# A second other order for the attention steps of a decoder layer, from the 81st step on

## The reference, cut to what matters

```python
x = x + self_attention(layernorm(x), w_qkv, w_out)      # x: (4, 1024, 256) fp32, 16 heads of 16
x = x + cross_attention(layernorm(x), ctx, mask, ...)   # ctx: (4, 77, 256), q, k, v with biases
x = x + ffn(layernorm(x), ...)                          # 704 wide, SiLU gate, values and weights rounded to 8 bits

# self_attention: windows of 128 queries, each over its own 128 keys and the 128 before, causal
scores = einsum('bhcqd,bhckd->bhcqk', qc, kcat) / HD ** 0.5
attn = softmax(where(mask, scores, -inf))
out = einsum('bhcqk,bhckd->bhcqd', attn, vcat) @ w_out
# cross_attention: softmax over 77 keys, masked by mask_SxS2_ik0
# ffn: the rounding scale of its input is max |layernorm(x)| over the whole tensor
```

## Time and profile before

| | us |
|---|---|
| median of 3 runs | 680.71 |
| lowest, highest | 676.21, 681.20 |
| the profiled execution | 682.17 |
| its span on the core | 680.4 |

### The profile page before, as it was taken

The page is one execution under the profiler, slowest core; times in us unless marked ns, Lnnn a source line. Parts: engine busy times, 40 slices in busy tenths (PEclk is TensorE's granted clock), DMA queues, the critical chain, the costliest instruction groups (busy, mean ns, idle before and its releaser), DMA issues.

```text
span 680.4 us, 20176 instructions
## 1 busy us (share of the span) xinstructions
PE 623.9 (92%) x8115; PEld 398.6 (59%) x8120; DVE 513.1 (75%) x984; ACT 403.1 (59%) x601; POOL 166.6 (24%) x215
## 2 busy tenths in 40 slices
PE   2999999999998999999999998999997999888885
PEld 2557575867665666566757664566754645333364
DVE  6698777777877767557866875677669778699897
ACT  3335666775674557566555466445354683899692
POOL 2004332432343210240242022123102011345300
PEclk9999999999999999999999998998999999999999
DMA  7744134562344243437323353434247340000024
GB/s 258 185 149 148 46 114 118 145 158 67 112 123 127 81 124 84 112 115 181 108 60 113 113 147 72 116 81 127 70 119 213 85 84 2 1 0 1 1 93 155
DMA packets 58266, 71.61 MB, mean 105 GB/s; under 512 B 23819, under 2 KB 35263, under 8 KB 58175
## 3 DMA queue, kind: packets, MB, share of 16 engines
q1 hardware_dynamic: 54495, 68.36, 36.1%
q10 hardware_dynamic: 3680, 1.97, 1.1%
HBM read 17.21 MB, written 4.69 MB: 32 GB/s over the span
## 4 chain that ended last, share of the span: by engine, by line
PE 64%; DVE 15%; SPq 6%; issue 5%; DMA 5%; ACT 4%; ACTq 0%; DVEq 0%
PE banks L493 41%; PE banks L688 7%; PE banks L608 5%; PE banks L699 4%; SPq L426 3%; DVE mtop L1158 3%; PE banks L551 2%; DVE tops L1370 2%; SPq L421 2%; ACT xnT L1034 1%; SPq L444 1%; DVE big L1363 1%; PE banks L769 1%; DVE parts L1345 1%; PE banks L611 1%
## 5 line engine op out<-in xcount | busy, mean ns | idle before, releaser
L493 PE MATMUL banks<-big 96*128 96x77 bf16 (+3 forms) x1348 | 160.2, 239 | 9.6 <-DMA big<-kparts 3.3
L1158 DVE TENSOR_REDUCE mtop<-banks 128x4 f32<-128x640 f32 (+3 forms) x128 | 127.3, 1020 | 39.8 <-PE banks L617 39.1
L493 PEld LDWEIGHTS banks<-big 99*128 99x128 bf16 (+2 forms) x1348 | 103.1, 102 | 77.5 <-issue 36.3
L1469 POOL TENSOR_SCALAR_AFFINE_SELECT big<-big 128x512 f32<-128x512 f32 x96 | 65.3, 680 | 231.7 <-ACT big L949 230.8
L949 ACT ACTIVATE big<-banks 128x1024 f32<-128x1024 f32 x96 | 96.9, 1028 | 41.5 <-PE banks L493 41.3
L493 PE MATMUL banks<-xnT,weights 128*128 128x512 f32 x192 | 91.5, 606 | 0.0
L608 PE MATMUL banks<-big 96*32 96x160 bf16 (+3 forms) x1792 | 69.9, 253 | 1.3 <-issue 0.8
L953 ACT ACTIVATE big<-banks 77x1024 f32<-77x1024 f32 x48 | 47.6, 1020 | 27.3 <-PE banks L493 25.4
L1162 DVE TENSOR_REDUCE mtop<-banks 128x8 f32<-128x616 f32 x64 | 49.3, 791 | 19.0 <-PE banks L493 18.5
L688 PE MATMUL banks<-big 128*17 128x256 f32 x768 | 57.9, 387 | 0.0
L962 ACT COPY oe<-banks 128x512 f32<-128x512 f32 x64 | 36.8, 588 | 32.1 <-DMA oTx<-oe 10.3
(11 more groups left out here) (173 smaller groups left out, 1216.6 us busy)
## 6 DMA issues: line engine op xcount, KB each, us to landing
big<-parts SPq DMA_DIRECT2D x285, 128.0 KB, 2.5
oc<-sums SPq DMA_DIRECT2D x15, 512.0 KB, 4.5
oTs<-oe SPq DMA_DIRECT2D x64, 64.0 KB, 2.4
out_dram<-oTs SPq DMA_DIRECT2D x16, 256.0 KB, 2.2
xs<-in_x_dram SPq DMA_DIRECT2D x3, 1024.0 KB, 6.2
big<-oe SPq DMA_DIRECT2D x32, 64.0 KB, 2.4
oTx<-oe SPq DMA_DIRECT2D x32, 64.0 KB, 2.3
xs<-in_x_dram SPq DMA_DIRECT2D x2, 512.0 KB, 6.4
```

Of the source, the lines that this page charges most:

```text
L493: return e.matmul(to[0:w], k[:, 0:w], q, start=start, stop=stop, skip_group_check=True)
L1158: e.tensor_reduce(M.rearrange("p (h c) -> p h c", h=4)[:, :, c], pair(p).rearrange("p j (s n) -> p (j s) n", s=2)[:, :, 0:160 + 32 * (c % 4)],
L1469: e.affine_select(out=P[:, :, 0:128], in_=P[:, :, 0:128], compare_op=ALU.is_ge, fill=0.0, base=0, pattern=[[0, 4], [1, 128]], channel_mult ...
```

## The change

The string `ORDER` is another from its 81st letter on. It has the same number of each letter, so every step is there once, and the steps of one letter keep their sequence. No other line changes. Banks, `pt` buffers, and the counts that semaphores are waited for follow from the order, by the same functions. Between whole-array and column-tile steps the new order changes 194 times. The first and the last lines of the diff:

```diff
 ORDER = (
-    "TTzfnnnnnRnnnRNlNnnqqcAcqqcncnMCfnVnMWVmmmmDmmmmnrqmcqtmcnBqmqnLsnRAsBmCccmWMVsvmMmVWNsTmFvvsrsNZqtm"
-    "mDvvvsmTmnvsesmqsvmngpvesmmcssvrsAvmnmCvmcvsntqgmqBcWscevmvVMpWmDvmWssMQeVmFAvdmrssmmgvsmKtvsmmvsnWq"
...
-    "vgimmquysvsveesmhrCcsvvutveuvAhdmxyqesycs2mysmYmpsvvhwitgvrveh22km3B4mmsmxses4r44v4o45t4oy4o5y5osp4m"
-    "v554memmeryiUuvvu5styysspsv5yeyuvvye5Y5vg5sssseue44v4vvvd455p5ibbxxUogyyowgjyyojypyojyyJYjJJJ6E5")
+    "TTzfnnnnnRnnnRNlNnnqqcAcqqcncnMCfnVnMWVmmmmDmmmmnrqmcqtmcnBqmqnLsnRAsBmCccmWMVsvWDANsmnVmvgvMFmsrTsn"
+    "ZmtqssvNvemvTmmmqssvpvmmvCnessWWmvmvccsrWBqscgqptvmmsmcvvWdsmmmmvvneWVnnssDVpegFmAmvMMssrmvsssvwvvsQ"
+    "KmtgKeiqmmqssvvCmmvccsKeqvsrRqtssvmvmvccsseemvLvmmvvmVMissVxmmMssNvssmvvrdmvtmTNpssvvmTmxvvmeKeqqBmm"
+    "ocwrcqDssqctcXooonsssvvssnnnngnvApvvnnCnsssvemmRvvmmXBVmmvmMDNpsssmgevvmmmTvssrMdVNmmqtTgpvmmnecqssv"
+    "vismssAevvnnwmmBrssgvvvchtssCmvmmvssedvmmvssenwnvvnssxVmvriMqqhsckvtsqmmvvvvxpcnsscqAmooRmmmreecvvsm"
...
+    "eqqtownctohhicgoonnnnnnnsRCsssssuANvvvesmhTvvNmemmrTpqtusxqcvBvvgpcdokymyooommmwssprUhPktmmeemmsysss"
+    "grvviehh1uuvvugessyyqCvvdvvAumyteemmcywqmircssxvt2ssvvvsyssp223mmmsYx444mUeehh444koo4r4yoomt5myyu5mm"
+    "5r5vivvveesBstsuuseevgyvvvsss444see4vp4pgvpy5y4yygvvYu555U5d55555ibbxxoyyoyyojywgyojyypjY6jJJJJE")
```

More of the change, by code:

```diff
@@ L34 @@
 ORDER = (
-    "TTzfnnnnnRnnnRNlNnnqqcAcqqcncnMCfnVnMWVmmmmDmmmmnrqmcqtmcnBqmqnLsnRAsBmCccmWMVsvmMmVWNsTmFvvsrsNZqtm"
-    "mDvvvsmTmnvsesmqsvmngpvesmmcssvrsAvmnmCvmcvsntqgmqBcWscevmvVMpWmDvmWssMQeVmFAvdmrssmmgvsmKtvsmmvsnWq"
-    "vmqvisesvKwccqsWmpvvnmsvCrsmecmtRqvsmsvmcssvgmmvvmseMeBVdvpKNssKLVMxrTwmvmsDsivmtNXsvvmqsgTvAmvmssvm"
-    "meqsspvxvrccqsovnenmcqocnBsXntvCmonnpsosmvvgmnvssesvmdvmnRvsDwsmvMNVemvTsrNnMVtqsmvvpmmensnvsmsvvegs"
-    "ATisCgBmvmvsmcmrvsdqsvtmhmpvcssmmvewsnvvAmemsmvsmssvvsvnCxhrmpsimktmmqgmBqvrvDnsgcmxsceqqvmnvcnvtsoR"
@@ L40 @@
[L40 to L44, removed]
@@ L45 @@
-    "vtehmeoonnonipsnrsonnhntsnBsRwhvmmmveANvgpCmgNBssTsevTrxqqccpodwtomoUgosmyvvuvvemmkeshysprtysP1svmyk"
-    "vgimmquysvsveesmhrCcsvvutveuvAhdmxyqesycs2mysmYmpsvvhwitgvrveh22km3B4mmsmxses4r44v4o45t4oy4o5y5osp4m"
-    "v554memmeryiUuvvu5styysspsv5yeyuvvye5Y5vg5sssseue44v4vvvd455p5ibbxxUogyyowgjyyojypyojyyJYjJJJ6E5")
+    "TTzfnnnnnRnnnRNlNnnqqcAcqqcncnMCfnVnMWVmmmmDmmmmnrqmcqtmcnBqmqnLsnRAsBmCccmWMVsvWDANsmnVmvgvMFmsrTsn"
+    "ZmtqssvNvemvTmmmqssvpvmmvCnessWWmvmvccsrWBqscgqptvmmsmcvvWdsmmmmvvneWVnnssDVpegFmAmvMMssrmvsssvwvvsQ"
@@ new lines @@
+    "KmtgKeiqmmqssvvCmmvccsKeqvsrRqtssvmvmvccsseemvLvmmvvmVMissVxmmMssNvssmvvrdmvtmTNpssvvmTmxvvmeKeqqBmm"
+    "ocwrcqDssqctcXooonsssvvssnnnngnvApvvnnCnsssvemmRvvmmXBVmmvmMDNpsssmgevvmmmTvssrMdVNmmqtTgpvmmnecqssv"
+    "vismssAevvnnwmmBrssgvvvchtssCmvmmvssedvmmvssenwnvvnssxVmvriMqqhsckvtsqmmvvvvxpcnsscqAmooRmmmreecvvsm"
+    "morsstoNCgtppsgBssvvvmvmmmeevvsssnvnmmDvvndnnssmmnnrpssqqgAitVvBemMmevmccnwTsssgevvvpNmkCCmvvmAsemsm"
+    "rTxsvvsstqqpccdggsqqpcvvcvvsmmsRmmwsmmmmeessivvvBNsTrrDsdvvvttsmmveemmvsssswmmvvmgNmVVprTMMixBqqesgt"
@@ new lines @@
+    "mvAevmhccvdssxsssvvCvmmowmmeevvmmosirsoqqssvvnnnhtccqpsnACsqghmmvevvvccpsmhommBsmemmrnDnhnsxsvvtVMgp"
+    "MVsospgdssyAvvveemmmvvvmBgsswkyoCpmmvpmmvrrqqgidtonssRotvveemmmNccAsssssevvmmTmvveyyssswNCpmvvmssvsr"
+    "uqixtTsvvvvksmmmcsyeevgmrsqscvvBvdtsysyssvvmmvwvveemmrssssktvvvvmmpmmgCieusssxsvgydAephYmmmmrBrvxvve"
+    "eqqtownctohhicgoonnnnnnnsRCsssssuANvvvesmhTvvNmemmrTpqtusxqcvBvvgpcdokymyooommmwssprUhPktmmeemmsysss"
+    "grvviehh1uuvvugessyyqCvvdvvAumyteemmcywqmircssxvt2ssvvvsyssp223mmmsYx444mUeehh444koo4r4yoomt5myyu5mm"
```

## The result

The new order takes 694.85 us (median of 14 runs, 682.5 to 707.5) where the order before takes 679.32 (14 runs on the same chip, 675.2 to 683.0): a ratio of 1.0127, 95% interval 1.0087 to 1.0168. The ratios in this document compare, for each kernel, only the runs within 1.5% of its fastest (6 of the 14 here); by the medians of all runs the new order is 2.3% slower, 15.5 us. Forecast were 671.0 us and a range of 663 to 681. The profiled execution of the new order took 699.74 us, span 698.0; it is 4.9 us above the median, and its mean granted clock, 0.953, is at the low end of the 14 runs (0.945 to 0.984). From here on a line of the new kernel is one higher than the same line before (L493 is L494).

A forecast was written before the change was run, and what follows sets the result against it. TensorE's work plus waits was taken to bound 45 to 557 us. 682.17 - 12.1 + 0.7 + 2.0 + 1.5 - 3.3 + 1.5 = 672.5, less 1.46 to the median: 671.0 us, range 663 to 681.

The forecast's parts named there:

- What bounds the kernel: From about 45 to 557 us, time is TensorE's work plus its waits: busy 493.7 of 512 us, waits 18.3.
- the price of a change: Whole-array to column-tile and back on TensorE: 0.22 us a pair; 51 fewer pairs, with cheaper projections, give -12.1 us.
- The SyncE queue is reordered with the rest: Loads on SyncE for all other jobs keep 7.5 us or more between qk and max; no cost added.
- Unknown new waits: 0: Nothing added for unforeseen waits; -5 to +5 us kept for the range.
- The clock: Rival: grouped steps make fewer, longer TensorE waits; five more falls to 1.2 GHz add 8.5 us, 679.5 us; chance 0.07.
- Readers +2.0: TensorE waits longer for ScalarE or VectorE to read PSUM banks before refilling: +2.0 us, bounds 0 and +6.
- held exps +1.5: ScalarE held at 24 scores whose pt buffer is freed by a later val: +1.5 us, bounds 0 and 13.0.
- Of other long chains ... the shortest are alike in both orders: Last val to out, out to turned, val to slot: 16.0 and 16.3 us for x2, 2.3 and 3.0 for the last.
- halved gain: Rival: TensorE's waits grow so that half of what is removed returns; 676 us, chance 0.18.
- Transfers -3.3: TensorE's two waits for cross-attention keys, at the first max of x0a and x0b, both go: -3.3 us.
- The end of attention +1.5: Around the last val: casts ahead of the last exp +1.2, ScalarE's work before broad +0.3, together +1.5 us.
- The cover +0.7: Last 57 us of attention, VectorE preparing FFN weights: six fewer changes hidden in waits, +0.7 us of gain lost.

The follow-up runs named there:

- e5: Old order plus 51 unread 32-column matmuls in column tiles, each between two whole-array steps: 692.18 us, ratio 1.0191 to the old order.
- e6: Control in the old order: the same 51 unread 32-column matmuls in the same places, on the whole array: 683.52 us, ratio 1.003.
- e15: New order with gate and up weights loaded at about 470 us, down behind x2b's second gather and x3a's small transfer: 679.1 us, ratio 0.9995 to the old order.
- e2: New order plus 14 unread 512-column matmuls in the wait before x3a's first score, transfer still late: 687.4 us, ratio 1.0048 to the old order.
- e16: Old order with gate and up weights loaded early, from 465.7 us, and down where all three stood: 678.91 us, ratio 1.0012 to the old order.
- e11: New order plus 14 unread matmuls before x3a's first score and 16 before three other waits, loads unmoved: 684.98 us, ratio 1.0048 to the old order.
- e12: New order with weights loads waiting for x3a's 24 KB transfer and placed behind x2b's second gather: 686.10 us, ratio 1.0027 to the old order.

## Why the prediction was wrong, point by point

**What bounds the kernel, and the price of a change: right.** TensorE's busy time fell by 11.2 us at full clock, where "down by about 10 to 12 us" was given as the sign. e5 against e6 measures the pair at 0.17 us by the medians, where 0.22 was taken and 0.18 was the lower bound, in other surroundings.

**The step that failed first: "The SyncE queue is reordered with the rest", with "Unknown new waits: 0".** I compared only the distance from qk to max for the keys. The loads of the feed-forward weights, the same five instructions, moved ahead of the 24 KB of x3a's maxes and further ahead of the gather of sums. The new order reaches x2b's last val 5.4 us sooner (502.9 us for 508.3), which is what opens the way for the loads; the small transfer came only 3.6 us sooner. m3t waits went from 0.3 to 5.5 us. I had read that queue only for what TensorE waited for before, not for what stands 0.7 us behind it. e15, which moves only the loads, is level with the order before: that shows what this step cost.

**The step that set the size: "The clock", five more falls at 1.7 us each.** The mechanism of that rival is what happened; two more falls were enough (five in the span for three), and its price per fall was wrong by far. I took the price from the 4 us around a fall that the old order recovers from in 3.4 us. Nor were the falls tied to the longest waits, as the prediction has it: before, they stand at waits of 2.09 and 1.41 us, and one of 1.98 us (at 211.8 us) passed without a fall. The new order's two falls lasted 20.5 and 34.1 us. In them a matmul pair of the cross scores takes 0.41 in place of 0.22 us. Over all runs the time goes with the mean granted clock: medians of 0.963 and 694.9 us in the new order, 0.994 and 679.1 in e15. The case had a chance of 0.07, and its 679.5 us were not enough. The rule of the Trainium skill that stood beside this rival (page "TensorE: Matmul & The Clock Gate", section "A second HAM failure mode: psum-queue depth-cycling"), that short idles between groups of matmuls cost throughput through the clock, speaks of swings; the two stretches here were long and steady, 20.5 and 34.1 us. How much of the loss is the low clock and how much the late transfer itself, only e2 tells, which leaves the transfer late and fills the wait: some 60% came back. Why the stretches lasted so long stays open.

**Readers +2.0, held exps +1.5: not too small together, but split wrongly.** Waits for exps grew by 5.2 us. Waits for maxes, which I had growing with the count of near places, fell by 3.4. So the two came to +1.8 against the +3.5 forecast. Which part of the 5.2 comes from the held exps and which from longer rows of scores I did not separate.

**The step that took the gain at full clock: "Of other long chains ... the shortest are alike in both orders", with nothing added.** Waits for x steps grew by 4.1 us, for transfers by 2.8 where -3.3 was forecast, and those without a named cause by 2.2: 9.1 us, against -3.3. With the readers and exps, and 1.5 less for the merging of maxes, 9.5 us came back. In size this is the halved gain, and more: nearly the whole of it. In its mechanism, the readers, it is not.

**Transfers -3.3: right as an item** (3.3 to 0.6 us), but other transfers took its place: parts and m3t, 4.7 us in e15 against 0.2 in e16. **The end of attention +1.5: right in direction**; from last val to broad it is 2.5 us more than before's 5.4 in e15, 1.6 of them by low clock, which that sum did not have. **The cover +0.7** can't be told from these.

Put together, at full clock up to the last val: -11.2 busy, +9.7 waits, +2.4 at the end gives about +0.9 (the two spans are 677.7 and 676.9 us), and e15 and e16 differ by 0.2 us in the median.

## What to carry to other kernels

When an order changes, list the large loads next to every small transfer that an engine waits for within 10 us, on all queues together, and see whether their order flips; here a difference of 2 us in who moved how far cost 15 us in the median. Do not price a clock fall by the falls that the kernel shows today: the same wait was followed by 3.4 us of low clock in one kernel and by 34.1 in another. And count waits and busy time apart: a change that makes a full engine's work shorter by 11 us, and puts 1216 letters in another order to do it, met new waits of nearly the same size.

## What the runs showed of the hardware that was not expected

- The clock stays at 1.2 GHz for 20.5 and 34.1 us although TensorE is busy almost all the time: 20.00 of 20 us in 550 to 570 us of the new order, at 0.50. In e11, 325 to 345 us, it is busy 20.00 of 20 us at 0.57. With twelve 512-column matmuls in the midst such a stretch lasted 6.8 us in place of 34.1 (one profile of each). In the old order's sequence of steps it ended by itself within 3.4 to 10.2 us.
- Not each wait lowers it: e15 has waits of 1.9, 1.7 and 1.6 us and stays at 1.00 up to its last val, while the new order's 1.56 us at 542.5 us, 10 us behind the end of a low stretch, was followed by the 34.1 one. The same wait, for xs, took 1.56 us in e2 and was followed by 3.4 us, and in e12 1.55 us (at 539.5 us, 9 us behind the end of a low stretch) and was followed by no fall. What tells them apart stays open.
- 24 KB on ScalarE's queue, issued in the midst of five loads of 2.1 MB on SyncE's, let TensorE go on 6.8 us after their issue; issued 0.7 us ahead of the first of them, 3.3 us.
